# Expert rows gathered over a slot map, results added back by DMA, and chunks of up and down projections that alternate in the last phase

## The reference

```python
x = x + gnn0(layernorm(x), src, dst)   # segment_sum of 50000 edges, then 256-512-1024-512-256 with batch norm and elu
x = x + ffn0(layernorm(x))             # 8 experts, the best 2 of a node, silu(x w1) * (x w3), then w2; hidden 682
x = x + gnn1(layernorm(x), src, dst)   # edge attention, 4 heads of 64
x = x + ffn1(layernorm(x))             # score = x wr; the best 1561 nodes get gelu(x w1 + b1) w2 + b2, times score; hidden 1024
```

```python
probs = softmax(flat @ router_w.T)
topk_probs, topk_idx = top_k(probs, 2)
topk_probs = topk_probs / (sum(topk_probs) + 1e-09)
gates = einsum('np,npe->ne', topk_probs, one_hot(topk_idx))
out = einsum('ne,nec->nc', gates, y)   # y: every expert's result
```

## Time and profile before

| | us |
|---|---|
| median of 3 runs | 2361.29 (2360.31 to 2362.19) |
| the profiled execution | 2358.71 |
| its span, first to last instruction | 2357.0 |
| TensorE busy | 1833.0 (78%) |
| VectorE busy | 1389.7 (59%) |
| GpSimd busy | 1338.6 (57%) |
| ScalarE busy | 663.1 (28%) |
| granted TensorE clock, mean | 0.796 of full speed |

### The profile page before, as it was taken

How to read it: one execution, slowest core, us unless ns; L and a number is a source line. 1 busy time by engine, 2 the same in 40 slices (tenths; PEclk the granted TensorE clock), 3 DMA queues, 4 the chain that set the end, 5 groups by cost and what they waited for, 6 DMA issues and landing times. The chain is left out here.

```text
span 2357.0 us, 37032 instructions
## 1 busy us (share of the span) xinstructions
PE 1833.0 (78%) x9586; PEld 1303.0 (55%) x9587; DVE 1389.7 (59%) x3211; ACT 663.1 (28%) x1302; POOL 1338.6 (57%) x1387
## 2 busy tenths in 40 slices
PE   2889889898897996604999999436887888884788
PEld 2677667674343455602666666235665665662466
DVE  7666644446555867671333333365777777776566
ACT  4000000002555656261333333112111111113663
POOL 3777777771777770084444444675777777772000
PEclk8655555658897998556999999757889889986899
DMA  7333333334003002622111111132111111112001
GB/s 230 105 105 103 105 105 105 105 105 145 1 1 56 1 1 76 217 78 59 36 36 39 37 36 36 50 87 68 28 28 29 28 28 28 28 28 6 1 1 55
DMA packets 109913, 142.46 MB, mean 60 GB/s; under 512 B 43751, under 2 KB 79463, under 8 KB 109855
## 3 DMA queue, kind: packets, MB, share of 16 engines
q0 software_dynamic: 60160, 86.81, 15.3%
q1 hardware_dynamic: 49695, 55.00, 7.8%
HBM read 112.44 MB, written 29.17 MB: 60 GB/s over the span
## 5 line engine op out<-in xcount | busy, mean ns | idle before, releaser
L497 PE MATMUL psA<-oh,G 128*128 128x128 f32 x1568 | 438.4, 443 | 67.8 <-DMA G<-xn_d,gat_i 34.3
L595 POOL DMA_INDIRECT rec_d<-rec,posd x392 | 391.7, 999 | 166.9 <-issue 124.5
L1515 POOL DMA_INDIRECT g<-tab_d,recs x416 | 394.9, 949 | 148.8 <-issue 126.4
L312 POOL DMA_INDIRECT G<-xn_d,gat_i x392 | 377.0, 962 | 146.9 <-issue 138.1
L497 PEld LDWEIGHTS psA<-oh,G 128*128 128x128 f32 x1568 | 345.8, 308 | 160.4 <-issue 97.0
L1664 PE MATMUL psS<-vv,oh 128*125 128x260 f32 x832 | 288.8, 494 | 91.3 <-DVE acc L1596 91.3
L840 PE MATMUL psZ<-z,W 128*128 (+1 forms) x1344 | 264.0, 359 | 26.0 <-DVE z L739 26.0
L1664 PEld LDWEIGHTS psS<-vv,oh 128*125 128x125 f32 x832 | 161.6, 226 | 188.9 <-DVE acc L1596 159.5
L447 DVE TENSOR_TENSOR accT<-accT,psA 128x256 f32 x392 | 164.8, 420 | 167.7 <-PE psA L497 141.7
L642 ACT ACTIVATE z<-psZ,vec 128x500 f32 (+2 forms) x112 | 70.8, 634 | 639.6 <-PE psZ L833 529.8
L840 PEld LDWEIGHTS psZ<-z,W 128*128 128x128 f16 x1344 | 124.5, 98 | 165.5 <-issue 38.3
(11 more groups left out here) (291 smaller groups left out, 2645.6 us busy)
## 6 DMA issues: line engine op xcount, KB each, us to landing
raw<-in_L_ffn_w SPq DMA_DIRECT2D x16, 682.0 KB, 10.5
xs_d<-zero SPq DMA_DIRECT2D x1, 7168.0 KB, 23.5
xs<-xs_d SPq DMA_DIRECT2D x56, 128.0 KB, 2.0
y_d<-yv POOLq DMA_DIRECT2D x56, 128.0 KB, 2.0
g<-tab_d,recs POOLq DMA_INDIRECT x416, 2.5
G<-xn_d,gat_i POOLq DMA_INDIRECT x392, 2.7
rec_d<-rec,posd POOLq DMA_INDIRECT x392
raw<-in_L_ffn_w SPq DMA_DIRECT2D x16, 384.0 KB, 10.3
```

The lines of the kernel that those rows point to most:

```text
L312: pool.indirect_dma_start(out=G[:, i, :], out_offset=None, in_=xn_d, in_offset=bass.IndirectOffsetOnAxis(ap=gat_i[:, t:t + 1], axis=0)).th ...
L497: last = nc.tensor.matmul(psA[i // 2][:, i % 2, h, :], G[:, i, 128 * h:128 * (h + 1)], oh[:, i, :], start=True, stop=True)
L595: pool.indirect_dma_start(out=rec_d.rearrange("p (t r) -> (p t) r", r=2), out_offset=bass.IndirectOffsetOnAxis(ap=posd[:, t:t + 1], axis=0 ...
L1515: pool.indirect_dma_start(out=g3[:, n % BODY, j, :], out_offset=None, in_=tab_d, in_offset=bass.IndirectOffsetOnAxis(ap=recs[:, t, 1:2], a ...
```

## The change

Records: `EDGES_EARLY` is 280, and two are left per tile. The 7 MB buffer `xs_d` and its zeroing are gone.

Routing: GpSimd stores the normalised rows `xn2` (ten DMAs) and `x2` (two) to DRAM in their natural order. `M`, `T`, `top` and `topi` now lie over `xn2` in memory. For each slot VectorE and TensorE find which node it holds and with which gate: for 10 (block, choice) pairs at a time VectorE compares the slot's tile (`oht`) and its place in the tile (`ohr`), multiplies by the three values of the pair (`valt`), and 10 matmuls add that up in `psM`; from this come `from_i`, `to_i` and `weight`. 12 of the 48 weight pieces are split by ScalarE beside the last 12 blocks of the router.

Expert loop: GpSimd fetches a tile's rows by an indirect gather (`fetch`, four buffers) and adds its results to `x2` in DRAM by an indirect DMA (`give`), each after the previous one has landed. The pass holds four tiles. The table stage loads `x2` back in five chunks.

Last FFN: per chunk eight ups, then the turns, then the four downs of the same chunk.

```diff
-        EDGES_EARLY = 224
+        EDGES_EARLY = 280
-                sp.dma_start(xs_d.rearrange("(t p) d -> p t d", p=128),
-                             zero[:, :].unsqueeze(1).to_broadcast([128, T2, D])).then_inc(s_zst, 16)
+                sp.dma_start(x2_d[N:N + 128, :], zero[:, :]).then_inc(s_zst, 16)
...
-                pool.wait_ge(s_slot, 1)
-                for b in range(NB):
-                    for k in range(K2):
-                        j = b * K2 + k
-                        pool.indirect_dma_start(
-                            out=xs_d, out_offset=bass.IndirectOffsetOnAxis(ap=slot_i[:, j:j + 1], axis=0),
-                            in_=xn2[:, b, :], in_offset=None).then_inc(s_scx, 16)
...
+                def fetch(t):
+                    if t >= XB:
+                        pool.wait_ge(s_xsT, t - XB + 1)
+                    pool.indirect_dma_start(
+                        out=xs[:, t % XB, :], out_offset=None, in_=xn2_d,
+                        in_offset=bass.IndirectOffsetOnAxis(ap=from_i[:, t:t + 1], axis=0)).then_inc(s_xs[t % XB], 16)
+
...
+                def give(t):
+                    i = t % 2
                     pool.wait_ge(s_yv, 1 + t + 1)
-                    pool.dma_start(y_d[t * 128:(t + 1) * 128, :], yv[:, i, :]).then_inc(s_yst[i], 16)
+                    if t:
+                        pool.wait_ge(s_yst[1 - i], 16 * ((t - 1) // 2 + 1))
+                    pool.indirect_dma_start(
+                        out=x2_d, out_offset=bass.IndirectOffsetOnAxis(ap=to_i[:, t:t + 1], axis=0),
+                        in_=yv[:, i, :], in_offset=None, compute_op=ALU.add).then_inc(s_yst[i], 16)
...
+                        if b >= NB - SOON:
+                            half_w(b - (NB - SOON))
...
-                    nc.scalar.activation(yv[:, i, :], psY[:, :], ACT.Copy, scale=1.0 / (WS * HS)).then_inc(s_yv, 1)
+                    nc.scalar.activation(yv[:, i, :], psY[:, :], ACT.Copy, scale=weight[:, bass.ds(t, 1)]).then_inc(s_yv, 1)
...
+                for n in range(SOON):
+                    half_w(n)
+                dve.wait_ge(s_xn2st, 160)
                 dve.wait_ge(s_lg, NB)
...
+                for n in range(NB * K2 // JC):
+                    js = slice(JC * n, JC * (n + 1))
+                    if n >= 2:
+                        dve.wait_ge(s_map, n - 1)
+                    nc.vector.tensor_tensor(oht[:, n % 2, :, :], iota[0:PB, 0:T2].unsqueeze(1).to_broadcast([PB, JC, T2]),
+                                            place3f[:, 1, js].unsqueeze(2).to_broadcast([PB, JC, T2]), ALU.is_equal).then_inc(s_val, 1)
+                    nc.vector.tensor_tensor(ohr[:, n % 2, :, :], iota[0:PB, :].unsqueeze(1).to_broadcast([PB, JC, 128]),
+                                            place3f[:, 0, js].unsqueeze(2).to_broadcast([PB, JC, 128]), ALU.is_equal).then_inc(s_valr, 1)
+                    dve.wait_ge(s_val, n + 1)
+                    nc.vector.tensor_tensor(valt[:, n % 2, :, :, :], oht[:, n % 2, :, :].unsqueeze(2).to_broadcast([PB, JC, 3, T2]),
+                                            vals[:, js, :].unsqueeze(3).to_broadcast([PB, JC, 3, T2]), ALU.mult).then_inc(s_valr, 1)
...
-                with loop(nc, pe, 0, T2 // 2 - 1) as g:
+                with loop(nc, pe, 0, T2 // XB - 1) as g:
+                    tiles(g * XB, g + 1, XB)
...
-                for j in range(NB * K2):
-                    if j >= 8:
-                        pool.wait_ge(s_res, j - 7)
-                    pool.indirect_dma_start(
-                        out=yg[:, j % 8, :], out_offset=None, in_=y_d,
...
+                nc.gpsimd.memset(acc[:, :, :], 0.0).then_inc(s_a0, 1)
...
                 for c in range(5):
...
-                        nc.vector.scalar_tensor_tensor(x2[:, b, :], yg[:, j % 8, :], gate[:, b, k:k + 1], x2[:, b, :],
-                                                       ALU.mult, ALU.add).then_inc(s_res, 1)
-                    dve.wait_ge(s_res, 5 * (c + 1) * K2)
+                    dve.wait_ge(s_x4[c], 32)
                     normalise(dve, ch, x2, xn3, c, s_v4, s_d4, s_n4)
...
+                    if c < 4:
+                        low_x(3 * c + 3)
+                        low_x(3 * c + 4)
+                    if c < 3:
+                        fold(c + 2)
+                    for b in range(b0, b0 + nb):
+                        lower(b)
+                        if c < 4 and b == b0 + 1:
+                            low_x(3 * c + 5)
+                        if c < 3 and b == b0 + 1:
+                            scales6(c + 2)
...
                     for m in range(FM):
                         up(c, m, n)
                         n += 1
-                        if c >= 2 and m % 2 == 1:
-                            down(b0 - CB + m // 2)
...
+                    if c < 4:
+                        turn6(3 * c + 3)
+                        turn6(3 * c + 4)
+                    for b in range(b0, b0 + nb):
+                        down(b)
+                        if c < 4 and b == b0 + 1:
+                            turn6(3 * c + 5)
```

More of the change, by code:

```diff
@@ L1001, in _ @@
+                pool.wait_ge(s_xn2st, 160)
+                pool.wait_ge(s_where, 1)
+                for t in range(XB):
+                    fetch(t)
+                pool.wait_ge(s_x2st, 32)
+                pool.wait_ge(s_zst, 16)
                 for t in range(T2):
-                    store(t, t % 2)
                     for j in range(PER_TILE):
                         record(pool, EDGES_EARLY + t * PER_TILE + j)
+                    if t + XB < T2:
+                        fetch(t + XB)
+                    give(t)
@@ new lines, in _ @@
+                ch.step(nc.vector.scalar_tensor_tensor(found[:, 3, :], found[:, 3, :], -1.0, found[:, 2, :], ALU.add, ALU.add))
+                ch.step(nc.vector.tensor_scalar(found[:, 2, :], v, 0.0, spare[:, :], ALU.is_equal, ALU.mult))
+                nc.vector.tensor_scalar(from_i[:, :], found[:, 3, :], 0.0, None, ALU.max)
+                ch.step(nc.vector.tensor_tensor(to_i[:, :], found[:, 3, :], found[:, 2, :], ALU.add))
+                dve.sem_inc(s_where, 1)
+                for n in range(SOON, X * PIECES):
+                    half_w(n)
@@ L1217, in _ @@
                 last.then_inc(s_tot, 1)
+                for n in range(NB * K2 // JC):
+                    pe.wait_ge(s_valr, 2 * n + 2)
+                    for j in range(JC):
+                        last = nc.tensor.matmul(psM.rearrange("p s t -> p (s t)"), ohr[:, n % 2, j, :],
+                                                valt[:, n % 2, j, :, :].rearrange("p s t -> p (s t)"),
+                                                start=(n == 0 and j == 0), stop=(n == NB * K2 // JC - 1 and j == JC - 1))
+                    last.then_inc(s_map, 1)
                 pe.sem_inc(s_up, 4)
@@ L1386, in _ @@
                 sp.dma_start(wx[:, :, NH:NH + OD], a["L1_gnn_W"].rearrange("(k p) n -> p k n", p=128)).then_inc(s_wlr, 16)
+                for c in range(1, 5):
+                    residual(c)
                 sp.wait_ge(s_one, 1)
@@ new lines, in _ @@
+                        if c < 4 and m in (3, 4, 5, 6, 7):
+                            logit(5 * c + m - 3)
+                        if c == 3 and m == 7:
+                            dve.wait_ge(ch.sem, ch.n)
+                            for b in range(20, NB):
+                                logit(b)
+                            dve.wait_ge(ch.sem, ch.n)
+                            dve.wait_ge(s_k6, 12)
+                            search(0)
+                        if c == 4 and m in (3, 7):
+                            search(5 + m // 4)
@@ L2033, in _ @@
+                for b in range(20, NB - 1):
                     finish(b)
-                for b in range(CHUNKS[-1][0], NB):
-                    lower(b)
-                    finish(b)
+                lower(NB - 1)
+                finish(NB - 1)
             @block.tensor
```

348 lines of the change are left out of this document (196 added, 152 removed).

## The result

| | before | after |
|---|---|---|
| median of 4 runs, us | 2361.74 | 2258.80 (2258.10 to 2263.02) |
| ratio, 95% interval | | 0.9567 (0.9551 to 0.9584) |
| profiled execution's span | 2357.0 | 2256.3 |

What follows compares the result with a forecast made beforehand. GpSimd's scatters set routing and its gathers the table stage, TensorE the experts; +12.5 - 28 - 12.4 - 4.4 - 53 - 18 = -103.3 took 2358.7 to 2255.4, plus 2.6 for the median: 2258 us, range 2236 to 2288.

Steps and rivals of the forecast that it cites:

- Records, +12.5: MLP stage, before routing: 56 more GpSimd records outlast 62.02 us of idle cover, so it ends 12.5 us later (+10 to +15).
- 8 us sooner than before and not 16: Sign at the expert loop's start: its first turn some 16 us before 1092, with the +12.5 in it.
- Routing, -28: Routing: scatters go, map steps of 3.85 us and 36 weight pieces in 33.1 follow; first turn at 1064.5 against 1092.68.
- rival B: Routing: VectorE waits for the stores of normalised rows behind the weight loads, up to +15 us, 2273; chance 0.09.
- Experts, -12.4 and -4.4: Expert stage: 13 fewer pass ends at 0.95 us each give -12.4; an earlier stage end gives -4.4.
- The tail's -4.4: End of expert stage: last give lands 4 us after issue, 1.2 for leaving the block; ends at 1504.6 against 1509.0.
- The give chain: Expert loop: each accumulating scatter waits for the previous landing, about 4.5 us, hidden by TensorE's tile up to about 7.0.
- Rival A: Expert loop: give landings set the pace, slower than before from 8.9 us; chance 0.04 in full, 0.05 in part.
- Table, -53: Table stage: 50 gathers and additions go, x2 returns in five chunks; 46 us against 98.5 (-45 to -57).
- Last FFN, -18: Last FFN: new order takes 192 us against 210, including three times 1.9 for low clock after stalls (-30 to -6).
- The stall: Last FFN: third down waits for the first lower, behind VectorE's fold and statistics; 4.5 us in chunks 0 to 2.
- rival C: Last FFN gains nothing: fold and ScalarE's chain give two stalls of 5 per chunk; 2276, or 2285 at 8; chance 0.10.

Runs made afterwards that it cites:

- e2: Changed kernel with 224 early records again and the 56 moved ones issued in the routing stage: 2254.3 us, ratio to before 0.9551.
- e11: Changed kernel with all 48 weight pieces split after the map, none beside the router: 2270.8 us, routing 124.3 against 116.3.
- e7: Changed kernel with GpSimd waiting for each give's landing right after its issue: 2321.0 us, expert stage 457.7.
- e8: Changed kernel with GpSimd waiting right after each give, which overwrites instead of adding (incomplete result): 2256.2 us, expert stage 395.6.
- e4 to e6: Three edits of the changed kernel's last FFN (196.0 us): fold and twice both moved, 187.7; only fold moved, 197.0; only twice moved, 194.9.
- e9: Changed kernel with the 56 records in routing, 25 ahead of the map and 31 behind the first four fetches: 2247.9 us, ratio to before 0.9521.

## Why the prediction came out, term by term

**Records, +12.5 forecast, +20.3 measured.** The step that failed is "56 cost 71 to 74 us plus about 1 for leaving the block". From 886.0 before to 963.4 after they cost 77.4, 4.4 more than the 73 in the sum. This has three parts. The last 55 records took 75.3 us, 1.37 each, since until VectorE's work of the MLP ended about every third of them had up to 1.47 us of issue in place of 0.97; with one more at 1.27 that is 3.5 above 73. GpSimd stood for 3.65 us behind its 225th record. And it had reached its 224th 2.8 us sooner than before. The stop behind the 225th record is in every profile of a kernel with 280 early records (3.65 to 5.57 us) and in none with 224, so it belongs to the change; most of what the end of the MLP stage varies by is this stop and the start of the stream. Its cause stays open.

Leaving the block is not 1.5 but 4.88 us when GpSimd is the last, which is the other 3.4. Before, at this border, it was not the last, and VectorE, which was, left in 0.3. But a row of before spoke against 1.5: at the end of the expert stage the last instruction on GpSimd was a record that ended at 1505.15, and

```profile
1508.92 0.14 POOL L1403 MEMSET row<- 125x25 f32 x1 [3.77 <-POOLq L122]
```

e2 shows that the whole 20 us are GpSimd's. For the same reason the first turn of the expert loop stands at 1084.65, 8 us sooner than before and not 16.

**Routing, -28 and -28.3.** Each step holds: copy 2.6 us later in the stage (2 forecast), map 3.88 a step (3.85), 36 pieces in 32.8 (33.1). The wait for the stores cost nothing, so rival B falls; e11 confirms the price of the early pieces.

**Experts, -12.4 and -4.4 forecast, -19.3 measured.** The pass end was mis-sized. I took 0.95 from 7.64 - 6.69, but 6.69 is itself the first tile behind a pass end; a tile with no end near it takes 6.56, so two-tile passes pay 7.64 + 6.69 - 13.12 = 1.21 for each end and four-tile passes 1.03: 27 x 1.21 - 13 x 1.03 = 19.3 in place of 12.4. From first to last turn the loop is 19.7 us shorter. The tail's -4.4 was not there: from the last turn to the next stage 28.5 us now, 28.2 before. Forecast were 5.2 us from the last give's issue to the next stage (4 and 1.2), measured are 10.0. GpSimd idles 8.41 us after its last give; by e7 2.6 of that is the landing, and the other 5.8 is again a late exit of GpSimd's (4.2 in e8 by the same sum, at most 3.77 before). Its cause stays open.

**The give chain.** 4.5 us forecast, 4.20 measured (e7). Rival A, with 8.9 as the point from which it decides, falls by a factor of two, and in the changed kernel no give waits for its forerunner. The rule of the Trainium skill ("DMA: Bandwidth & Descriptors", rules for kernel authors) that each accumulation has to wait for the one before therefore costs nothing in this loop, since TensorE's tile is 6.8; e7 shows what it costs when GpSimd waits at once and its own tile grows to 8.0: 60.7 us in the stage.

**Table, -53 and -59.7.** The mechanism is right, three sizes were each too long: the first chunk 5.0 us in (6), a chunk 5.0 (5.2), and from the fifth layernorm to the end 14.1 us (17.4 + 2). That last stretch was 17.7 before, at a granted clock of 0.69, and is 14.1 at 0.96. Of the 3.6 between them 2.3 lie ahead of ScalarE's last row, which the clock can explain but no run isolates, and 1.3 behind it. The bound of -57 was too near.

**Last FFN, -18 and -14.1.** The stall stands where it was forecast, before the third down, 4.75 us in chunks 1 and 2 and 5.55 in chunk 0 (4.5). The downs behind it take 8.27, 7.12 and 8.38 us for two in place of 5.41, at a granted clock of 0.65, 0.75 and 0.63: 7.5 us in all, where I allowed three times 1.9. Even so chunks 1 and 2 (28.3 and 29.6) are 2.3 shorter than the forecast with its allowance. What was too small is chunk 0 with 35.0 (30.8 and 1.9) and chunks 3 and 4 with 25.2 each (24, 23), in which TensorE waits 2.52, 1.50 and 1.36 us for VectorE beside the search. The reason given for the stall was half of it: the fold ahead of the lowers is one of two chains that end within a microsecond of each other, the other being ScalarE's (statistics, root, norm, twice, table load). I had put that in rival C only as something that makes it worse. e4 to e6 show that neither alone is the bound.

So the sum for the span missed by 2.6 us only because +7.8 and +3.9 met -2.5 and -6.7 (routing and attention differ by less than 1), and the 2.6 us added for the median then covered that. That the total fits to 1 us is luck. The direction of each term but the tail's is not: the waits that set routing, the expert loop and the table stage are the ones that the prediction named, while it had GpSimd's exits, the stop in its records and ScalarE's chain in the last FFN missing or too small.

## What to carry to other kernels

Work moved "into idle time" of an engine is free only up to the barrier, and there it costs what the next stage waits for, the exit of that engine included; put it where the engine waits for data, and look at what the other engines do to it there. Where two chains end within a microsecond or so, an experiment with one edit shows almost nothing: make the edits apart and together. When a forecast of several terms comes out to 1 us, compare it stage by stage before believing it.

## What the runs showed of the hardware

- GpSimd's issue of an indirect DMA was held up beside some of VectorE's work: one issue took 19.42 us in e2, the length of the map's five steps (19.44) of 125x560 to 125x1680 elements with two SBUF inputs, while the record begun 0.4 us ahead of the map took 0.96; beside the splitting of weights a record took 1.52 us in place of 0.97 to 1.02 (e9). VectorE's own times did not change. The Trainium skill, "GPSIMD Engine Reference", key points, says that GpSimd shares its SBUF interfaces with VectorE and names two SBUF inputs as a case of contention; the traces agree, and show that it can be a full block. The splitting has two SBUF inputs as well, and why it costs a record only half a microsecond no run here shows.
- GpSimd left the MLP stage 4.88 us after its last indirect DMA was issued (after), VectorE 0.3 us after its last instruction (before, 947.74 to 948.07).
- In all nine profiles of kernels with 280 early records GpSimd's stream of them stopped for 3.65 to 5.57 us behind the 225th; in those with 224 it has no such stop.
- From the start of the issue of an accumulating scatter of 128 rows of 1 KB to GpSimd's next instruction behind its landing it took 4.20 us, of a plain one 2.69 (e7, e8; DMA share 0.21 and 0.13 over the loop). In the measure of the earlier trace rows the medians are 3.9 and 2.4; the plain scatters of before took 3.9 there, beside the loading of weights.
- The end of a hardware loop's pass on TensorE cost 1.21, 1.03 and 1.28 us with bodies of two, four and eight tiles; the other ends inside these loops lie within 0.1 us of that.
